# Rotary partners of q and k: found by VectorE across the halves of the partitions, in place of products with swapped weights

## The chip, the cores and the metric

The kernel runs on one core of a Trainium2 chip. The metric is the device time of one execution in microseconds, as the median of several runs. A trace of one profiled execution stands beside it.

## What is computed

Three layers in a row on 4 x 1024 tokens of 256 features (float32): a mixture of experts at half weight, attention without a mask, with 16 query heads and 4 key/value heads of 16 features each, and the mixture of experts again with the same weights. What the change touches is the rotary embedding of q and k:

```python
def _rotate_half(x):
    x1, x2 = jnp.split(x, 2, axis=-1)
    return jnp.concatenate([-x2, x1], axis=-1)
q = jnp.einsum('bsh,oh->bso', x, Wq).reshape(b, s, NH, HD).transpose(0, 2, 1, 3)
k = jnp.einsum('bsh,oh->bso', x, Wk).reshape(b, s, NKV, HD).transpose(0, 2, 1, 3)
q = q * cos + _rotate_half(q) * sin
k = k * cos + _rotate_half(k) * sin
```

So feature d of a head needs its partner, feature d + 8 or d - 8 of the same head.

## The kernel before

The tokens go in 8 groups of 512 (GROUP). Each mixture layer is a row of slots: a slot d is one step of the loop `for d in range(-1, SLOTS + ...)` that every engine runs in its own version, 24 slots to a group (PER_GROUP), 192 to a layer, 384 in all. In a slot TensorE (PE) does 12 matmuls for the gate and 12 for the up projection (`gate_or_up`, L1070) and 12 for the down projection (`down`, L1088). ScalarE (ACT) takes the tanh of the gate (L587), VectorE (DVE) forms the gated product (`gated` L834, `product` L842), GpSimd (POOL) weighs it (L514), ACT rounds it to float16 (L594) and POOL takes the rest (L519).

Other work is laid into these slots by tables. `VISIT` gives each slot from d = 64 (FIRST) to about d = 310 two, sometimes three, visits of the attention: in a visit PE makes two score products for the maximum (L1100), which DVE reduces (L857), and two for the exponential (L1112), which ACT takes (L617). Every second visit (odd v, `quad_at`) also begins with the products with the values (L1131). `EVENTS` gives slots an event: transposes, logits, and the joins, which make q, k and v of one group. The joins of group g stand in slots 24 (g + 1) + 8 and on (P_JOIN = 8): before the change seven of them, q block 0, q block 0 with swapped weights, q block 1, the same swapped, k, k swapped, v. A q or k join is 6 matmuls of 512 columns (L1042 for q, L1045 for k). Each is an event at the end of its slot on PE and on DVE. The joins of g = 0 and 1 lie ahead of the attention, those of g = 2 to 7 inside it.

An event's product needs a PSUM bank. Ahead of the attention it is B_O, which is used by nothing else there. Inside it the bank is B_U, that of the up projection (`event_bank`), so that the up half of the next slot first waits until DVE has taken the join (`pe.wait_ge(*taken[b])` in `gate_or_up`). Between the two PE has one gate half (12 matmuls) and one visit.

q and k then take this way: DVE writes `rb`, ACT rounds it to `qo_hi` (`rope_high`, L601), POOL takes the rest (`rope_low`, L501), SP stores both to HBM (`store_block`), and for each unit u of batch and key head SP loads them back (`load`, L410 and L414), 12 DMAs to a unit, each for 16 partitions. The queue of SP is in order: spread (the weights of the experts, L372), store_block, store_values, load, rows. The first load stands at d = 64, and PE's first visit needs it in the same slot.

DVE's program in a slot is: visit, gated, product, visit, then a piece of a layer norm if the slot has one (`norm_of`, in slots 9 to 12 of a group: 4 bn_stats, bn_aggr, the Newton step, the 4 normalising ones), then the event.

Of the kernel before, what the change touches and what calls it, by code (L numbers as in the profile page):

```python
# [16 lines left out]
P = 128  # L17
# [15 lines left out]
QB = 2  # L33
# [79 lines left out]
JOINS = 2 * (QB + 1) + 1  # L113
# [53 lines left out]
def build(nc, x, wgu, wd, wg, wq, wk, wv, wo, ident_c, ktab_c, kneg_c, out):  # L167
    with ExitStack() as ctx:
# [14 lines left out]
        WQ = [sb(f"WQ{h}", [P, KT, 2 * QB, P], F16) for h in range(2)]  # L183
        WK = [sb(f"WK{h}", [P, KT, 2, K_ROWS], F16) for h in range(2)]
# [14 lines left out]
        pad = sb("pad", [P, 1])  # L199

# [36 lines left out]
        n_small = [KT * EXPERTS, KT * 2 * QB * P, KT * 2 * K_ROWS, KT * KV * HD, KT * HID]  # L237
# [109 lines left out]
        def _(sp):  # L347
# [53 lines left out]
            def load(u):  # L401
# [47 lines left out]
            for d in range(-1, SLOTS + 3):  # L449
# [35 lines left out]
        def _(pool):  # L485
# [51 lines left out]
            for d in range(-1, SLOTS + 2):  # L537
# [3 lines left out]
                if 1 <= k <= GROUPS and s in (10, 12, 14):  # L541
                    rope_low(k - 1, s // 2 - 5)
# [19 lines left out]
        def _(act):  # L562
# [33 lines left out]
            def rope_high(g, blk):  # L596
                n, rows = 3 * g + blk, P if blk < QB else K_ROWS
                act.wait_ge(j_taken, JOINS * g + 2 * blk + 2)
# [53 lines left out]
            for d in range(-1, SLOTS + 2):  # L652
# [7 lines left out]
                if 1 <= k <= GROUPS:  # L660
                    if s == 6:
                        rows_high(norm_of_join(k - 1))
                    if s in (10, 12, 14):
                        rope_high(k - 1, s // 2 - 5)
# [16 lines left out]
        def _(dve):  # L681
# [125 lines left out]
            def join(g, piece, bank):  # L807
                dve.wait_ge(j_done, JOINS * g + piece + 1)
                J = PS[:, bank, :]
                if piece < JOINS - 1:  # L810
                    blk, swapped = divmod(piece, 2)
                    n, m = P if blk < QB else K_ROWS, 3 * g + blk
# [484 lines left out]
```

## Time and profile before

| | |
|---|---|
| median of 3 runs | 2366.85 us (2366.6 to 2366.93) |
| profiled execution | 2365.77 us, its span 2364.0 us |
| PE busy | 2279.1 us, 96% of the span |
| DVE busy | 1570.8 us, 66% |
| ACT busy | 1236.7 us, 52% |
| POOL busy | 1050.9 us, 44% |

The busy time of an engine is the time in which one of its instructions runs. PE's own matmuls overlap, so that the price of a matmul on the path is the distance from one start to the next and not its duration. An engine that is idle costs nothing unless PE waits for it.

### The profile page before, as it was taken

To read this page: it belongs to the slowest core of one execution; us is meant where nothing else is said; L and a number is where in the kernel's file an instruction comes from. 1 tells how busy PE (TensorE), PEld (TensorE's weight loads), DVE (VectorE), ACT (ScalarE), POOL (GpSimd) and SP (SyncE) were. 2 spreads that over 40 slices of the span, in tenths; PEclk is the share of its full clock that TensorE was granted. 3 is DMA by queue.
4 is the path that set the end of the run, shared out by engine and by line. 5 is a ranking of instruction groups with operands and counts; after the bars stand their busy time and mean duration, and the time that the engine had idled before them with its cause. 6 is when DMAs were issued, how large, how long until landed. Compare 5 with 4: busy or idle time off the path is not lost.

```text
span 2364.0 us, 48461 instructions
## 1 busy us (share of the span) xinstructions
PE 2279.1 (96%) x19616; PEld 1517.4 (64%) x19616; DVE 1570.8 (66%) x3107; ACT 1236.7 (52%) x1966; POOL 1050.9 (44%) x863
## 2 busy tenths in 40 slices
PE   0899999999999999999999999999999999999999
PEld 0788875555555556556555555555655665688887
DVE  7656558877777777777777776776776763354543
ACT  3333332466665666666566566656666656633332
POOL 0666663443443443344334343433433434366665
PEclk9999999999999999999999999999999999999999
DMA  5210111011011011001101001010010000011010
GB/s 203 77 36 29 36 48 49 10 26 41 17 31 42 15 34 30 27 22 41 29 19 51 20 22 36 23 33 19 22 30 22 13 30 19 15 33 29 19 38 19
DMA packets 96343, 80.24 MB, mean 34 GB/s; under 512 B 40308, under 2 KB 88692, under 8 KB 95736
## 3 DMA queue, kind: packets, MB, share of 16 engines
q1 hardware_dynamic: 95976, 77.11, 11.4%
q8 instruction: 155, 2.54, 0.4%
q14 instruction: 68, 0.56, 0.1%
q10 hardware_dynamic: 144, 0.03, 0.0%
HBM read 64.25 MB, written 12.85 MB: 33 GB/s over the span
## 4 chain that ended last, share of the span: by engine, by line
PE 92%; DVE 6%; issue 1%; SPq 0%; ACT 0%; DMA 0%; POOL 0%; POOLq 0%; DVEq 0%; ACTq 0%
PE PS L1070 42%; PE PS L1088 21%; PE PS L1100 11%; PE PS L1131 11%; PE PS L1042 2%; DVE arena L857 1%; PE PS L1112 1%; PE PS L1017 1%; PE PS L1045 1%; PE PS L1172 1%; PE PS L1158 1%; DVE arena L834 0%; DVE amax L698 0%; PE PS L1026 0%; DVE WGU L709 0%
## 5 line engine op out<-in xcount | busy, mean ns | idle before, releaser
L1070 PE MATMUL PS<-XT,WGU 128*128 128x256 f16 x9216 | 1117.1, 274 | 48.9 <-DVE WGU L709 32.0
L1070 PEld LDWEIGHTS PS<-XT,WGU 128*128 128x128 f16 x9216 | 875.0, 98 | 279.8 <-issue 131.9
L519 POOL TENSOR_TENSOR arena<-arena 128x512 f16<-128x512 f32 x384 | 447.3, 1165 | 1197.4 <-ACT arena L594 1197.4
L857 DVE TENSOR_REDUCE arena<-PS 128x1 f32<-128x512 f32 x1024 | 657.7, 684 | 369.6 <-PE PS L1100 367.6
L617 ACT ACTIVATE arena<-PS,fac 128x512 f32<-128x512 f32 x1024 | 647.4, 685 | 236.2 <-PE PS L1112 234.9
L587 ACT ACTIVATE arena<-PS,fac 128x512 f32<-128x512 f32 x384 | 264.0, 688 | 760.6 <-PE PS L1070 760.6
L1088 PE MATMUL PS<-WD,arena 128*128 128x256 f16 x4608 | 568.0, 273 | 1.8 <-POOL arena L519 1.6
L1088 PEld LDWEIGHTS PS<-WD,arena 128*128 128x128 f16 x4608 | 432.3, 98 | 141.5 <-issue 89.9
L514 POOL TENSOR_TENSOR arena<-arena 128x512 f32<-128x512 f32 x384 | 492.9, 1284 | 47.0 <-DVE arena L842 45.6
L834 DVE SCALAR_TENSOR_TENSOR arena<-arena,PS 128x512 f32<-128x512 f32 x384 | 261.0, 680 | 281.2 <-ACT arena L587 280.7
L1100 PE MATMUL PS<-arena 48*128 48x512 f16 x1024 | 311.9, 382 | 7.4 <-DMA arena<-k_scratch 4.6
L1112 PE MATMUL PS<-arena 50*128 50x512 f16 x1024 | 308.6, 381 | 0.0
L842 DVE SCALAR_TENSOR_TENSOR arena<-arena,PS 128x512 f32<-128x512 f32 x384 | 263.7, 687 | 33.8 <-PE PS L1070 17.9
L1131 PE MATMUL PS<-arena 128*32 128x512 f32 x2048 | 272.7, 605 | 0.0
L594 ACT ACTIVATE arena<-arena 128x512 f16<-128x512 f32 x384 | 241.3, 628 | 6.1 <-POOL arena L514 6.1
L1100 PEld LDWEIGHTS PS<-arena 48*128 48x128 f16 x1024 | 58.1, 94 | 269.1 <-issue 210.6
L575 ACT ACTIVATE XT<-PS 128x1024 f16<-128x1024 f16 x48 | 49.2, 1024 | 57.7 <-PE PS L1017 57.7
L1131 PEld LDWEIGHTS PS<-arena 128*32 128x32 f32 x2048 | 40.3, 108 | 53.9 <-issue 29.0
L1112 PEld LDWEIGHTS PS<-arena 50*128 50x128 f16 x1024 | 56.8, 94 | 21.0 <-issue 17.8
L1017 PE MATMUL PS<-ident,XS 128*128 128x128 f16 x384 | 30.2, 223 | 20.4 <-ACT XS L570 15.7
L496 POOL TENSOR_TENSOR XS<-XN,XS 128x1024 f16<-128x1024 f32 x23 | 49.0, 2130 | 0.0
L737 DVE TENSOR_SCALAR XN<-X,mv,rstd 128x256 f32<-128x256 f32 x96 | 48.7, 567 | 0.0
(115 smaller groups left out, 835.0 us busy)
## 6 DMA issues: line engine op xcount, KB each, us to landing
arena<-ce_scratch SPq DMA_DIRECT2D x256, 128.0 KB, 3.3
arena<-wgu SPq DMA_DIRECT2D x2, 3072.0 KB, 16.1
arena<-q_scratch SPq DMA_DIRECT2D x96, 64.0 KB, 2.2
arena<-ktab_c SPq DMA_DIRECT2D x16, 256.0 KB, 4.1
q_scratch<-arena SPq DMA_DIRECT2D x32, 128.0 KB, 1.7
out<-X SPq DMA_DIRECT2D x8, 512.0 KB, 3.0
X<-wd SPq DMA_DIRECT2D x1, 3072.0 KB, 26.3
X<-x SPq DMA_DIRECT2D x1, 3072.0 KB, 15.4
```

What stands on the lines that cost most here:

```text
L514: pool.tensor_tensor(t, t, c, ALU.mult).then_inc(w_done, 1)
L519: pool.tensor_tensor(hs[1][:, d % HS, :], tw[d % 2], hs[0][:, d % HS, :], ALU.subtract).then_inc(lo_done, 1)
L587: act.activation(z_f, PS[:, B_G, :], ACT.Tanh, scale=F_TANH).then_inc(z_done, 1)
L617: act.activation(pex[:, v % RING * 2 + half, :], PS[:, B_EXP + half, :], ACT.Exp, scale=F_EXP).then_inc(exp_done, 1)
L834: dve.scalar_tensor_tensor(z_f, z_f, 1.0, PS[:, B_G, :], ALU.add, ALU.mult).then_inc(v_done, 1)
L842: dve.scalar_tensor_tensor(tw[d % 2], z_f, G_U_UP, PS[:, B_U, :], ALU.mult, ALU.mult).then_inc(t_done, 1)
L857: dve.tensor_reduce(mx[:, half * REP * QT + c:half * REP * QT + c + 1], PS[:, B_MAX + half, :], AX_X, ALU.max).then_inc(max_taken, 1)
L1070: ins = pe.matmul(PS[:, b, j * HALF_G:(j + 1) * HALF_G], WGU[w][:, kt, part * CHUNKS + c + j, :], XT[r][:, k % 2, kt, half * HALF_G:(half ...
L1088: ins = pe.matmul(PS[:, B_Y, i * HID:(i + 1) * HID], hs[r][:, d % HS, at:at + P], WD[w][:, d % PER_HALF * 2 + j, :], start=(first and j == ...
L1100: pe.matmul(PS[:, B_MAX + half, :], qst[64 * par:64 * par + 48, slot, i, t * P:(t + 1) * P], kst[64 * par:64 * par + 48, slot, half * 512: ...
L1112: pe.matmul(PS[:, B_EXP + n % 2, :], kst[64 * par:64 * par + 50, slot, k * P:(k + 1) * P], qst[64 * par:64 * par + 50, slot, head // 2, ha ...
L1131: ins = pe.matmul(PS[32 * head:32 * head + 32, B_O, :], vst[:, u % 2, k, :], pex[:, (2 * q + r // 2) % RING * 2 + r % 2, :], start=(k == 0 ...
```

## The change

The swapped products go. The rows of Wq and Wk are laid out so that the first halves of the heads of a block lie in the lower half of the partitions and the second halves in the upper one; a partner is then 64 partitions away (32 for k). DVE multiplies by the cosine as before, makes the two partner halves from the other half of the partitions into a new tile `turned` in SBUF, and adds. Seven joins become four, in slots 8 to 11; rope_high and rope_low move to slots 9, 10, 11, the stores to slots 10, 11, 12 (and 13 for v). Since a head's features now lie in two places of the scratch, each load becomes 24 DMAs of 8 partitions in place of 12 of 16. WQ and WK are half as wide, and so are their transfer and their splitting into high and low halves at the start.

```diff
-JOINS = 2 * (QB + 1) + 1
+JOINS = QB + 2
@@
-        WQ = [sb(f"WQ{h}", [P, KT, 2 * QB, P], F16) for h in range(2)]
-        WK = [sb(f"WK{h}", [P, KT, 2, K_ROWS], F16) for h in range(2)]
+        WQ = [sb(f"WQ{h}", [P, KT, QB, P], F16) for h in range(2)]
+        WK = [sb(f"WK{h}", [P, KT, K_ROWS], F16) for h in range(2)]
@@
+        turned = sb("turned", [P, GROUP])
@@ load
-                    for r, h in enumerate((0, 0, 1)):
-                        sp.dma_start(qst[64 * par + 16 * r:64 * par + 16 * r + 16, slot, :, :],
-                                     q_d[h, b, 64 * j:64 * j + 64, :]
-                                     .rearrange("(i q d) n -> q d i n", i=2, q=2)[par]).then_inc(q_in[slot], 16)
-                    for r, h in enumerate((0, 1, 0)):
-                        sp.dma_start(kst[64 * par + 16 * r:64 * par + 16 * r + 16, slot, :],
-                                     k_d[h, b, 16 * j:16 * j + 16, :]).then_inc(q_in[slot], 16)
+                    for s in range(2):
+                        at = j // 2 * P + 64 * s + 32 * (j % 2)
+                        for r, h in enumerate((0, 0, 1)):
+                            to = 64 * par + 16 * r + 8 * s
+                            sp.dma_start(qst[to:to + 8, slot, :, :], q_d[h, b, at:at + 32, :]
+                                         .rearrange("(i q d) n -> q d i n", i=2, q=2)[par]).then_inc(q_in[slot], 16)
+                        for r, h in enumerate((0, 1, 0)):
+                            to = 64 * par + 16 * r + 8 * s
+                            sp.dma_start(kst[to:to + 8, slot, :],
+                                         k_d[h, b, 32 * s + 8 * j:32 * s + 8 * j + 8, :]).then_inc(q_in[slot], 16)
@@ SP's program
-                    if s in (11, 13, 15):
-                        store_block(k - 1, s // 2 - 5)
-                    if s == 15:
+                    if s in (10, 11, 12):
+                        store_block(k - 1, s - 10)
+                    if s == 13:
                         store_values(k - 1)
@@ join on DVE
-                    if not swapped:
-                        if blk == 0:
-                            dve.wait_ge(tab_in, 32 * (g + 1))
-                        if m:
-                            dve.wait_ge(qo_lo_done, m)
-                        dve.scalar_tensor_tensor(rb[0:n, :], J[0:n, :], HALF, kcos[0:n, :], ALU.mult, ALU.mult)\
-                           .then_inc(j_taken, 1)
-                        dve.wait_ge(j_taken, JOINS * g + piece + 1)
-                    else:
-                        link(dve.scalar_tensor_tensor(J[0:n, :], J[0:n, :], HALF, ksin[0:n, :], ALU.mult, ALU.mult))
-                        dve.tensor_tensor(rb[0:n, :], rb[0:n, :], J[0:n, :], ALU.add).then_inc(j_taken, 1)
+                    link.many((
+                        dve.scalar_tensor_tensor(rb[0:n, :], J[0:n, :], HALF, kcos[0:n, :], ALU.mult, ALU.mult),
+                        dve.scalar_tensor_tensor(turned[0:n // 2, :], J[n // 2:n, :], -HALF, ksin[n // 2:n, :],
+                                                 ALU.mult, ALU.mult),
+                        dve.scalar_tensor_tensor(turned[n // 2:n, :], J[0:n // 2, :], HALF, ksin[0:n // 2, :],
+                                                 ALU.mult, ALU.mult)))
+                    dve.tensor_tensor(rb[0:n, :], rb[0:n, :], turned[0:n, :], ALU.add).then_inc(j_taken, 1)
```

How instructions move is seen best in the programs of the engines. On DVE, around the first joins of group 0 (the tiles `kcos`, `ksin` and `rb` are parts of `arena`, PS is PSUM), there stood before:

```order
L818 SCALAR_TENSOR_TENSOR arena<-PS,arena 128x512
L834 SCALAR_TENSOR_TENSOR arena<-arena,PS 128x512
L842 SCALAR_TENSOR_TENSOR arena<-arena,PS 128x512
L741 BN_STATS stats<-X 128x6 x4
L822 SCALAR_TENSOR_TENSOR PS<-PS,arena 128x512
L823 TENSOR_TENSOR arena<-arena,PS 128x512
```

and there stands now, in the same two slots:

```order
L821 SCALAR_TENSOR_TENSOR arena<-PS,arena 128x512
L822 SCALAR_TENSOR_TENSOR turned<-PS,arena 64x512
L824 SCALAR_TENSOR_TENSOR turned<-PS,arena 64x512
L826 TENSOR_TENSOR arena<-arena,turned 128x512
L837 SCALAR_TENSOR_TENSOR arena<-arena,PS 128x512
L845 SCALAR_TENSOR_TENSOR arena<-arena,PS 128x512
L745 BN_STATS stats<-X 128x6 x4
L821 SCALAR_TENSOR_TENSOR arena<-PS,arena 128x512
L822 SCALAR_TENSOR_TENSOR turned<-PS,arena 64x512
```

A join takes one or two instructions of DVE before and four now, and DVE gives the bank back behind the fourth; the add, which read PSUM, now reads SBUF alone.

On PE, from the last join of q to the v join of group 0, there stood before:

```order
L1042 MATMUL PS<-XT,WQ 128x512 x6
L1070 MATMUL PS<-XT,WGU 128x256 x24
L1088 MATMUL PS<-WD,arena 128x256 x12
L1045 MATMUL PS<-XT,WK 64x512 x6
L1070 MATMUL PS<-XT,WGU 128x256 x24
L1088 MATMUL PS<-WD,arena 128x256 x12
L1045 MATMUL PS<-XT,WK 64x512 x6
L1070 MATMUL PS<-XT,WGU 128x256 x24
L1088 MATMUL PS<-WD,arena 128x256 x12
L1051 MATMUL PS<-WV,XT 128x64 x24
```

and now:

```order
L1044 MATMUL PS<-XT,WQ 128x512 x6
L1072 MATMUL PS<-XT,WGU 128x256 x24
L1090 MATMUL PS<-WD,arena 128x256 x12
L1047 MATMUL PS<-XT,WK 64x512 x6
L1072 MATMUL PS<-XT,WGU 128x256 x24
L1090 MATMUL PS<-WD,arena 128x256 x12
L1053 MATMUL PS<-WV,XT 128x64 x24
```

The v join comes three slots earlier, and three slots of the group have no join.

On SP, from the stores of group 1 to the first load, there stood before (ten more rows of 3 DMAs follow up to the end of unit 2):

```order
L390 DMA q_scratch<-arena 128x512 x4
L372 DMA arena<-ce_scratch 32x4x256 x4
L392 DMA k_scratch<-arena 64x512 x2
L399 DMA v_scratch<-arena 128x4x32 x4
L410 DMA arena<-q_scratch 16x2x1024 x3
L414 DMA arena<-k_scratch 16x1024 x3
```

and now:

```order
L391 DMA q_scratch<-arena 128x512 x4
L393 DMA k_scratch<-arena 64x512 x2
L400 DMA v_scratch<-arena 128x4x32 x4
L373 DMA arena<-ce_scratch 32x4x256 x4
L414 DMA arena<-q_scratch 8x2x1024 x3
L418 DMA arena<-k_scratch 8x1024 x3
```

The stores have moved ahead of the spread, which now lies between them and the load, and the load has twice as many DMAs, each of half the size.

## Rows read from the trace of the kernel before

**Rows 1.** The page: busy us of the engines; the chain that ended last by engine.

```profile
PE 2279.1 (96%) x19616; PEld 1517.4 (64%) x19616; DVE 1570.8 (66%) x3107; ACT 1236.7 (52%) x1966; POOL 1050.9 (44%) x863
...
PE 92%; DVE 6%; issue 1%; SPq 0%; ACT 0%; DMA 0%; POOL 0%; POOLq 0%; DVEq 0%; ACTq 0%
```

**Rows 2.** Waits of PE: who, for whom, us in total, times, longest.

```profile
PE PS L1100 <- DMA arena<-k_scratch: 4.6, 1, 4.6
...
PE PS L1070 <- DVE arena L823: 3.4, 3, 1.6
```

**Rows 3.** Timeline of PE ahead of the attention: start us, length us, what.

```profile
203.56 1.46 PE L1042 MATMUL PS<-XT,WQ 128*128 128x512 f16 x6
204.85 2.78 PE L1070 MATMUL PS<-XT,WGU 128*128 128x256 f16 x24
...
208.78 1.46 PE L1042 MATMUL PS<-XT,WQ 128*128 128x512 f16 x6
...
230.24 1.48 PE L1045 MATMUL PS<-XT,WK 128*64 128x512 f16 x6
231.65 0.61 PE L1070 MATMUL PS<-XT,WGU 128*128 128x256 f16 x4
```

**Rows 4.** Groups of instructions on DVE: busy us, mean ns.

```profile
L822 DVE SCALAR_TENSOR_TENSOR PS<-PS,arena 128x512 f32<-128x512 f32 x16 | 11.2, 699 | 2.9 <-PE PS L1042 2.6
...
L823 DVE TENSOR_TENSOR arena<-arena,PS 128x512 f32<-128x512 f32 x16 | 11.0, 686 | 0.5
...
L822 DVE SCALAR_TENSOR_TENSOR PS<-PS,arena 64x512 f32<-64x512 f32 x8 | 5.5, 692 | 11.2 <-PE PS L1045 11.2
```

**Rows 5.** Timeline inside the attention: a join, then a visit without values.

```profile
638.22 1.46 PE L1042 MATMUL PS<-XT,WQ 128*128 128x512 f16 x6
...
639.78 0.70 DVE L822 SCALAR_TENSOR_TENSOR PS<-PS,arena 128x512 f32<-128x512 f32 x1 [0.40 <-PE PS L1042]
640.52 0.69 DVE L823 TENSOR_TENSOR arena<-arena,PS 128x512 f32<-128x512 f32 x1
...
641.45 1.49 PE L1070 MATMUL PS<-XT,WGU 128*128 128x256 f16 x12
```

**Rows 6.** Timeline of PE: a join, and the up products behind a visit with values.

```profile
477.29 1.46 PE L1042 MATMUL PS<-XT,WQ 128*128 128x512 f16 x6
...
481.53 1.49 PE L1070 MATMUL PS<-XT,WGU 128*128 128x256 f16 x12
```

**Rows 7.** Timeline: a join that DVE takes late, and PE's wait.

```profile
653.72 1.46 PE L1042 MATMUL PS<-XT,WQ 128*128 128x512 f16 x6
...
657.08 0.70 DVE L822 SCALAR_TENSOR_TENSOR PS<-PS,arena 128x512 f32<-128x512 f32 x1
...
658.64 1.47 PE L1070 MATMUL PS<-XT,WGU 128*128 128x256 f16 x12 [1.62 <-DVE arena L823]
```

**Rows 8.** Timeline: DVE with two SBUF inputs beside a running POOL.

```profile
253.49 1.27 POOL L514 TENSOR_TENSOR arena<-arena 128x512 f32<-128x512 f32 x1
253.66 1.24 DVE L773 TENSOR_TENSOR pr<-pr,r 128x128 f32<-128x128 f32 x1
```

**Rows 9.** Timeline of SP and PE around the first load.

```profile
336.10 1.48 PE L1045 MATMUL PS<-XT,WK 128*64 128x512 f16 x6
...
345.53 1.39 SPq L410 DMA_DIRECT2D arena<-q_scratch  x3
346.54 1.47 PE L1070 MATMUL PS<-XT,WGU 128*128 128x256 f16 x12
...
352.64 0.59 PE L1100 MATMUL PS<-arena 48*128 48x512 f16 x2 [4.63 <-DMA arena<-k_scratch]
353.16 2.72 PE L1070 MATMUL PS<-XT,WGU 128*128 128x256 f16 x12
```

**Rows 10.** Splitting of weights at the start, by width.

```profile
L709 DVE SCALAR_TENSOR_TENSOR WQ<-arena,up,WQ 128x1024 f16<-128x1024 f32 x1 | 1.3, 1285 | 0.0
...
L709 DVE SCALAR_TENSOR_TENSOR WO<-arena,up,WO 128x512 f16<-128x512 f32 x1 | 0.8, 752 | 0.0
```

More of the change, by code:

```diff
@@ L236, in build @@
         n_gu, n_d = KT * 2 * CHUNKS * P, CHUNKS * HID
[L237 removed]
+        n_small = [KT * EXPERTS, KT * QB * P, KT * K_ROWS, KT * KV * HD, KT * HID]
         st_gu, st_g, st_q, st_k, st_v, st_o = carve([(n, F32) for n in [n_gu] + n_small])
@@ L540, in _ @@
                     low(d)
-                if 1 <= k <= GROUPS and s in (10, 12, 14):
-                    rope_low(k - 1, s // 2 - 5)
+                if 1 <= k <= GROUPS and s in (9, 10, 11):
+                    rope_low(k - 1, s - 9)
                 if d + 1 < SLOTS:
@@ L597, in rope_high @@
                 n, rows = 3 * g + blk, P if blk < QB else K_ROWS
-                act.wait_ge(j_taken, JOINS * g + 2 * blk + 2)
+                act.wait_ge(j_taken, JOINS * g + blk + 1)
                 if n >= 2:
@@ L662, in _ @@
                         rows_high(norm_of_join(k - 1))
-                    if s in (10, 12, 14):
-                        rope_high(k - 1, s // 2 - 5)
+                    if s in (9, 10, 11):
+                        rope_high(k - 1, s - 9)
                 if 0 <= k < PREPS - 1:
@@ L810, in join @@
                 if piece < JOINS - 1:
-                    blk, swapped = divmod(piece, 2)
-                    n, m = P if blk < QB else K_ROWS, 3 * g + blk
-                    if not swapped:
-                        if blk == 0:
-                            dve.wait_ge(tab_in, 32 * (g + 1))
-                        if m:
-                            dve.wait_ge(qo_lo_done, m)
-                        dve.scalar_tensor_tensor(rb[0:n, :], J[0:n, :], HALF, kcos[0:n, :], ALU.mult, ALU.mult)\
-                           .then_inc(j_taken, 1)
-                        dve.wait_ge(j_taken, JOINS * g + piece + 1)
-                    else:
-                        link(dve.scalar_tensor_tensor(J[0:n, :], J[0:n, :], HALF, ksin[0:n, :], ALU.mult, ALU.mult))
-                        dve.tensor_tensor(rb[0:n, :], rb[0:n, :], J[0:n, :], ALU.add).then_inc(j_taken, 1)
+                    n, m = P if piece < QB else K_ROWS, 3 * g + piece
+                    if piece == 0:
+                        dve.wait_ge(tab_in, 32 * (g + 1))
+                    if m:
+                        dve.wait_ge(qo_lo_done, m)
+                    link.many((
[5 more added lines that the diff above has]
+                    dve.tensor_tensor(rb[0:n, :], rb[0:n, :], turned[0:n, :], ALU.add).then_inc(j_taken, 1)
                 else:
@@ L1037, in join @@
                 if piece < JOINS - 1:
-                    blk, swapped = divmod(piece, 2)
                     for m, (a, b) in enumerate(PASSES):
                         for kt in range(KT):
-                            if blk < QB:
+                            if piece < QB:
                                 ins = pe.matmul(PS[:, bank, :], WQ[a][:, kt, piece, :], XT[b][:, slot, kt, :],
@@ L1044, in join @@
                             else:
-                                ins = pe.matmul(PS[0:K_ROWS, bank, :], WK[a][:, kt, swapped, :], XT[b][:, slot, kt, :],
+                                ins = pe.matmul(PS[0:K_ROWS, bank, :], WK[a][:, kt, :], XT[b][:, slot, kt, :],
                                                 start=(m == 0 and kt == 0), stop=(m == 2 and kt == KT - 1))
@@ L1143, in visit @@
                         pe.wait_ge(const_rows, 32)
-                    pe.wait_ge(q_in[u % QKV], 192 * (u // QKV + 1))
+                    pe.wait_ge(q_in[u % QKV], 384 * (u // QKV + 1))
                 if 0 <= v < VISITS and v % FILLS == 0:
@@ L1249, in rope_tables @@
     cos, sin = np.cos(ang).T.astype(np.float32), np.sin(ang).T.astype(np.float32)
-    sin = np.concatenate([-sin[:HD // 2], sin[HD // 2:]])
-    return np.stack([np.tile(cos, (8, 1)), np.tile(sin, (8, 1))])
+    cos, sin = cos[:HD // 2], sin[:HD // 2]
+    return np.stack([np.tile(cos, (16, 1)), np.tile(sin, (16, 1))])
 def layouts(a):
-    swap = (np.arange(HD) + HD // 2) % HD
     def on_partitions(w):
@@ L1264, in layouts @@
     down = a["L0_ffn_down_proj"].transpose(0, 2, 1).reshape(-1, HID)[rows].reshape(CHUNKS, P, HID)
-    q = a["L0_attn_Wq"].reshape(HEADS, HD, HID)
-    k = a["L0_attn_Wk"].reshape(KV, HD, HID)
+    q = a["L0_attn_Wq"].reshape(QB, HEADS // QB, 2, HD // 2, HID).transpose(0, 2, 1, 3, 4)
+    k = a["L0_attn_Wk"].reshape(KV, 2, HD // 2, HID).transpose(1, 0, 2, 3)
     return {
@@ L1271, in layouts @@
         "wg": on_partitions(a["L0_ffn_gate_weight"]),
-        "wq": on_partitions(np.stack([q.reshape(QB, P, HID), q[:, swap].reshape(QB, P, HID)], axis=1)
-                            .reshape(-1, HID)),
-        "wk": on_partitions(np.concatenate([k.reshape(-1, HID), k[:, swap].reshape(-1, HID)])),
+        "wq": on_partitions(q.reshape(-1, HID)),
+        "wk": on_partitions(k.reshape(-1, HID)),
         "wv": on_partitions(a["L0_attn_Wv"]),
```

## The prediction, made before the changed kernel ran

> **What bounds the kernel now.** I read the page first. PE is busy for 96% of the span and holds 92% of the chain that ended last; the other engines are at 44 to 66% [rows 1]. Then the list of PE's waits: apart from the start of the program, where PE waits for the weights to be split, it waits for hardly anything. Two entries are touched by the change: one wait of 4.6 us for the first load of q and k, and three waits, 3.4 us together, for the add that ends a swapped join on DVE [rows 2]. So nearly all of what PE no longer does comes off the time, unless it is given back as new waits, and the question is what PE meets where the joins now stand. For this I read the timeline around joins, once ahead of the attention and at several groups inside it.
>
> **What is removed from PE.** A slot ahead of the attention shows the price: the join of q starts at 203.56 and the gate products at 204.85, so a q join is worth 1.29 us; for k it is 231.65 - 230.24 = 1.41 us [rows 3]. (The durations, 1.46 and 1.48 us, overlap with what follows and are not the price.) I take the same price inside the attention. Two q joins and one k join go in each of 8 groups: 8 x (2 x 1.29 + 1.41) = **-31.9 us**. The three waits for L823 lay behind swapped q joins, which exist no more: **-3.4 us**.
>
> **What is added on DVE.** A join is now three multiplications out of PSUM and an add. Of the multiplications two have 64 (32) partitions and write into the other half. The nearest rows say that the number of partitions does not count (699 ns for 128, 692 ns for 64 [rows 4]); that the written half differs from the read one is shown by no row. Below, I take no surcharge. Above, I take twice the time, +0.7 us for each of the two. I use no surcharge, since the rows of both sizes are nearest in kind. With 0.70 us each, the small gap of 0.04 us between dependent ones (639.78 + 0.70 to 640.52 [rows 5]) and 0.69 us for the add, the four last 3 x 0.70 + 0.04 + 0.69 = 2.83 us. DVE as such has room: 8 x 3 more instructions are 8 x 3 x 0.69 = 16.6 us beside 1570.8 us of 2364. It is the latency that counts.
>
> **New waits inside the attention.** There the join holds the bank of the up products. In the slot of [rows 5] DVE starts 1.56 us behind PE's start of the join (it waited 0.40 us for it), is done at 641.21, that is 2.99 us behind the start, and PE comes to the up products at 3.23 us. With four instructions DVE is done at 1.56 + 2.83 = 4.39, and PE needs about 0.14 us to see it (657.81 + 0.69 = 658.50 would be the end of the add, PE goes on at 658.64 [rows 7]). The wait is then 4.53 - 3.23 = 1.3 us where the visit in between has no values. Where it has, PE comes only at 481.53 - 477.29 = 4.24 us [rows 6], and the wait is 0.3 us if DVE is on time. It is not always: the second join stands behind the four bn_stats, and in front of it DVE had 0.40 us of idle time here [rows 5] and no more in the other groups, so that the 2.1 us that the first join now adds are passed on in part; my estimate is 0.4 us more for the second joins with values, and nothing more for those without, since there PE itself is held by 1.3 us. By the table of visits, of the 18 joins of q and k inside the attention 7 are followed by a visit without values and 11 by one with: 7 x 1.3 + 11 x 0.3 + 3 x 0.4 = 13.6 us. Two joins stand in slots with three visits and one group (the last) has two events to a slot; there DVE was late already (the worst case of before is 3.36 us behind PE's start [rows 7]), and I add 3 us for them. **+16.6 us**. Bounds: if DVE is never late and the multiplications overlap a little, 8 us; if it is 1 us later at each of the 18, 35 us.
>
> **Ahead of the attention** the four instructions lie in a bank of their own. PE's slot with a join is 208.78 - 203.56 = 5.22 us [rows 3]; DVE needs 2.83 for the join and, at 0.69 each for this width [rows 4], 1.4 for gated and product, which leaves 1.0 us; the largest piece of a norm takes somewhat more than that, but in one slot only. What is behind the join on DVE is the gated product, which PE wants only two halves later. I take **0**; without that cover it would be 0.5 us in each of two groups.
>
> **The first load.** Before, the last k join starts at 336.10; the load begins at 345.53, takes 0.46 us of SP's queue for each DMA (1.39 for 3), and PE, which could have gone on at 346.54 + 1.47 = 348.01, goes on at 352.64 [rows 9]. Now the k join stands three slots earlier, against PE's need: it gains 3 x 3.93 = 11.8 us (204.85 to 208.78 is such a slot without its join [rows 3]). Against it, the load is 24 DMAs: 12 x 0.46 = 5.5 us more, and the spread of 4 DMAs (4 x 0.46 = 1.9 us) now lies in between. The load lands 352.64 - 336.10 + 5.5 + 1.9 = 23.9 us behind the k join, and PE needs it at 11.9 + 11.8 = 23.7 us. DVE's longer join may add 0.5 us. So of the 4.63 us some 0.5 stay: -4.1 us. Behind the long idle time PE also ran slowly: 12 gate matmuls took 2.72 us in place of 1.47 [rows 9]; with 0.5 us of idle time I expect none of this, -1.3 us. **-5.4 us**, between 0 (if DMAs of half the size cost more than the row says) and -6. The later loads (units 3 to 15) take 5.5 us longer on SP but are issued nine slots ahead of need (by the tables; five for unit 4), each longer than 3.93 us; they and the spreads queued behind them stay covered.
>
> **The start.** The split of WQ is 512 wide in place of 1024: 1285 - 752 = 0.53 us [rows 10], that of WK some 0.13. The search for the maxima shrinks by as much, and may or may not be hidden behind POOL's first reduction. **-1.0 us**, between -0.6 and -2.
>
> **The sum** is -31.9 - 3.4 + 16.6 + 0 - 5.4 - 1.0 = -25.1 us. The profiled execution took 2365.77 us, and would take 2340.7; the median of the runs is 1.1 us above it, so 2341.8 us. I give **2341.5 us**, 1.0% faster.
>
> **The lock between DVE and POOL.** The add used to read PSUM and now reads rb and turned, both in SBUF. The trace shows what that can mean: a tensor_tensor of 128 columns with two SBUF inputs took 1.24 us and ended at 254.90, 0.14 us behind the POOL instruction that was running [rows 8], while L823, with 512 columns but PSUM as one input, takes 0.69 us in the mean [rows 4]. If every add inside the attention met the start of a POOL instruction of 1.27 us, that would be 18 x 1.2 = 22 us more. In the slots that I looked at POOL is idle 3.7 to 4.4 us behind PE's start of a join (its weighing ends before DVE's turn, the rest comes later), so I put nothing of it in the sum beyond the bound. The Trainium skill (SBUF — State Buffer, on the shared port pair) states that a DVE instruction with two SBUF inputs and a GpSimd instruction that reads SBUF exclude each other for the whole instruction, whichever starts first; by that rule the change buys PE time with a DVE instruction that can be shut out, and if it were always shut out the time would be 2363 us; the trace agrees with the rule at this row.
>
> **The rivals.**
> - *Four instructions with little wait, as above*: 2331 to 2352 us. Chance 0.68.
> - *The adds are shut out by POOL* in many slots, or DVE drags its lateness from join to join: 2352 to 2364. For it speaks [rows 8] and that DVE was late before at three joins; against it, that POOL is idle in most of these moments. Central time 2358. Chance 0.13.
> - *Hardly any new wait*: the multiplications overlap, and DVE catches up: 31.9 + 3.4 + 6 + 2 - 8 = 35 us, 2331 and below. Against it, that PE comes at 3.23 us and three multiplications alone end at 3.66. Chance 0.07.
> - *Writing into the other half costs double*: 1.4 us more at each of 18 joins, 25 us: no change, 2367. No row speaks for it. Chance 0.05.
> - *The clock of PE falls at the new waits*, the case on the other side: after the idle 4.63 us of the first load 12 matmuls took 1.25 us longer [rows 9]. If that happened behind each of the 18 joins, for two such stretches each, it would be 18 x 2 x 1.25 = 45 us, 2387 us; it decides from 0.7 us a join on. Against it: behind the 1.62 us of idle time in [rows 7] the 12 matmuls took 1.47 us, as always, and the new waits are shorter than that. Chance 0.04, and 0.03 for other losses.
>
> **How the numbers follow.** About 0.2%, 4.7 us, is what a measurement of this kernel can tell from no change. Faster: 0.68 + 0.07 + 0.13 = 0.88, with a little of the doubled write 0.89; within 0.2%: 0.05; slower: 0.06. The range leaves out the last two rivals, half of the third and the upper half of the second: 2329 to 2357 us.
>
> **What the profile will show.** L1042 and L1045 (now L1044 and L1047) with 96 and 48 matmuls; the two cross-half multiplications at about 0.69 us each; among PE's waits one group that dwarfs the old ones, gate or up products waiting for the add of the join, some 15 us in 10 to 18 cases, the longest about 2 to 3 us; the wait for the first load at 0 to 1.5 us and no slow stretch behind it; adds of 0.6 to 0.7 us, the longer ones each beside a POOL instruction. I would be wrong if the cross-half writes are much dearer, if the wait for the load stays as it was because half-sized DMAs are no cheaper to land, or if DVE's lateness reaches other waits of PE, those for the maxima (L857) above all.

## The result: 1.2% faster, and the profile after

The changed kernel took 2338.36 us in the median (2336.99 to 2339.75) against 2366.72 us for the kernel before on the same chips, a ratio of 0.988 (95% interval 0.9864 to 0.9896). The profiled execution took 2338.99 us with a span of 2336.9 us, 27.1 us less than the 2364.0 of before. The forecast was 2341.5 us.

The page of the changed kernel (span, busy time by engine, shares of the chain):

```profile
span 2336.9 us, 48308 instructions
...
PE 2247.6 (96%) x19472; PEld 1504.5 (64%) x19472; DVE 1579.8 (68%) x3131; ACT 1236.0 (53%) x1966; POOL 1051.5 (45%) x863
...
PE 91%; DVE 7%; issue 1%; ACT 0%; DMA 0%; POOL 0%; POOLq 0%; DVEq 0%; ACTq 0%
```

PE lost 144 matmuls and 31.5 us of busy time against [rows 1], and is still the bound. PE's waits (who, for whom, us in total, times, longest):

```profile
PE PS L1072 <- DVE arena L826: 11.2, 14, 2.2
...
PE PS L1102 <- DVE arena L860: 2.2, 10, 0.3
PE PS L1072 <- DVE arena L830: 1.9, 2, 1.2
```

The wait for the load and that for L823, both in [rows 2], are gone. In their place stand 14 waits for the add of a join (L826) and two for the v join (L830), 13.1 us together, all inside the attention. Two waits of 0.36 us for X (L852), ahead of the attention, are new as well. What one of them is made of shows in the timeline, DVE and PE around the first join of the fourth group, a slot without values as in [rows 5]:

```profile
614.28 0.69 DVE L821 SCALAR_TENSOR_TENSOR arena<-PS,arena 128x512 f32<-128x512 f32 x1 [1.64 <-PE PS L1044]
615.01 0.69 DVE L822 SCALAR_TENSOR_TENSOR turned<-PS,arena 64x512 f32<-64x512 f32 x1
615.73 0.69 DVE L824 SCALAR_TENSOR_TENSOR turned<-PS,arena 64x512 f32<-64x512 f32 x1
616.45 0.69 DVE L826 TENSOR_TENSOR arena<-arena,turned 128x512 f32<-128x512 f32 x1
```

```profile
612.79 1.46 PE L1044 MATMUL PS<-XT,WQ 128*128 128x512 f16 x6
...
617.29 1.47 PE L1072 MATMUL PS<-XT,WGU 128*128 128x256 f16 x12 [1.19 <-DVE arena L826]
```

DVE starts 1.49 us behind the start of the join, is done at 617.14, and PE goes on 0.15 us later, 1.19 us late. The two multiplications that write into the other half take what any other of that width takes.

The first load (SP and PE), against [rows 9]:

```profile
328.59 0.95 SPq L414 DMA_DIRECT2D arena<-q_scratch  x3
329.58 0.97 SPq L418 DMA_DIRECT2D arena<-k_scratch  x3
```

```profile
338.34 1.47 PE L1072 MATMUL PS<-XT,WGU 128*128 128x256 f16 x12
339.75 0.60 PE L1102 MATMUL PS<-arena 48*128 48x512 f16 x2
```

A DMA of half the size takes SP 0.33 us in place of 0.46 (from one row to the next, for 3 DMAs), and PE comes to its first visit without waiting. SP is done with the 24 DMAs of the first unit at 337.70. Before the change PE went on 1.5 us behind the end of SP's last DMA for that unit; with the same delay the load is done some 0.5 us ahead of the visit at 339.75 (an estimate from these rows). One place is new: in the sixth group DVE takes the second join late, PE is idle for 2.21 us, and runs slowly behind it. PE's timeline, and PE's busy time and granted clock (1.00 is full speed, 2.4 GHz) in that stretch and the next:

```profile
967.95 2.72 PE L1072 MATMUL PS<-XT,WGU 128*128 128x256 f16 x12 [2.21 <-DVE arena L826]
```

```profile
967.95:971.60 3.65, 3.65 (x20) 1.78 (x20) 2.34 (x4) 0.52 (x1) 2.07 (x3) 0.57 0.21 72
971.60:974.00 2.40, 2.40 (x21) 1.34 (x18) 1.71 (x8) 1.26 (x2) 1.20 (x1) 1.00 0.00 0
```

**Where the 27.1 us are.** Removed products -31.9; waits for L823 -3.4; the load's wait -4.6 and the slow stretch behind it some -1.6; the start -0.6 (the first gate products begin at 55.82 in place of 56.38); new waits for joins +13.1, for X +0.7; the slow stretch at 968 us, 3.65 us at 0.57 of full speed, +1.6. The sum is -26.7 us. The start is uncertain by more than its size: in the traces of the changed kernel and its variants the first gate products begin between 55.36 and 57.25 us. What is the same in all of them is PE's wait for the split of the weights, 31.3 to 31.4 us in place of 32.0.

### The profile page after: what moved, and what is told of

Its sections match the earlier page's. It is cut to its first block, busy times and chain, and to the rows that moved or that the text cites. A ratio compares the mean times of both kernels' runs of the same rounds, so it can differ in the third digit from the quotient of the medians.

```text
span 2336.9 us, 48308 instructions
## 1 busy us (share of the span) xinstructions
PE 2247.6 (96%) x19472; PEld 1504.5 (64%) x19472; DVE 1579.8 (68%) x3131; ACT 1236.0 (53%) x1966; POOL 1051.5 (45%) x863
## 4 chain that ended last, share of the span: by engine, by line
PE 91%; DVE 7%; issue 1%; ACT 0%; DMA 0%; POOL 0%; POOLq 0%; DVEq 0%; ACTq 0%
PE PS L1072 43%; PE PS L1090 22%; PE PS L1102 11%; PE PS L1133 11%; PE PS L1114 1%; DVE arena L860 1%; PE PS L1020 1%; PE PS L1174 1%; PE PS L1044 1%; PE PS L1160 1%; PE PS L1047 0%; DVE arena L826 0%; DVE turned L824 0%; DVE turned L822 0%; DVE arena L821 0%
## 5 line engine op out<-in xcount | busy, mean ns | idle before, releaser
L1072 PE MATMUL PS<-XT,WGU 128*128 128x256 f16 x9216 | 1117.4, 274 | 57.5 <-DVE WGU L713 31.4
L860 DVE TENSOR_REDUCE arena<-PS 128x1 f32<-128x512 f32 x1024 | 658.1, 685 | 352.7 <-PE PS L1102 351.1
L837 DVE SCALAR_TENSOR_TENSOR arena<-arena,PS 128x512 f32<-128x512 f32 x384 | 261.2, 680 | 278.5 <-ACT arena L591 278.0
L845 DVE SCALAR_TENSOR_TENSOR arena<-arena,PS 128x512 f32<-128x512 f32 x384 | 263.8, 687 | 34.1 <-PE PS L1072 17.9
L741 DVE TENSOR_SCALAR XN<-X,mv,rstd 128x256 f32<-128x256 f32 x96 | 43.6, 515 | 0.0
```

The lines of the kernel that those rows point to most:

```text
L837: dve.scalar_tensor_tensor(z_f, z_f, 1.0, PS[:, B_G, :], ALU.add, ALU.mult).then_inc(v_done, 1)
L845: dve.scalar_tensor_tensor(tw[d % 2], z_f, G_U_UP, PS[:, B_U, :], ALU.mult, ALU.mult).then_inc(t_done, 1)
L860: dve.tensor_reduce(mx[:, half * REP * QT + c:half * REP * QT + c + 1], PS[:, B_MAX + half, :], AX_X, ALU.max).then_inc(max_taken, 1)
L1072: ins = pe.matmul(PS[:, b, j * HALF_G:(j + 1) * HALF_G], WGU[w][:, kt, part * CHUNKS + c + j, :], XT[r][:, k % 2, kt, half * HALF_G:(half ...
```

## Experiments

The theory: the gain is that of the removed products and of the load that is no longer late, and what is given back is the time for which a join holds the bank of the up products. The rivals: the lateness of DVE as such is what costs; the two cross-half multiplications are free or, at the other end, cost their full time; the place of the joins does not matter. The waits and timelines are those of one profiled execution of each kernel, which is not always near its median; where that matters the text says so. All of these kernels were timed beside the kernel before, which took 2366.55 to 2366.95 us in the median.

### The changed kernel again

> The changed kernel once more, beside the three variants that follow, so that differences of a few us can be read on one chip. Any theory: 2336 to 2340 us, and among PE's waits again some 11 us for the add that ends a q or k join and 2 us for the v join.

2338.9 us (2337.09 to 2339.78), with the same waits for joins: L826 11.2 us in 14 cases, L830 1.9 us in two. It is the measure for the others.

### The bank back behind the third multiplication

```diff
-                    link.many((
+                    for ins in (
                         ...
-                                                 ALU.mult, ALU.mult)))
+                                                 ALU.mult, ALU.mult)):
+                        ins.then_inc(j_free, 1)
+                    dve.wait_ge(j_free, 3 * m + 3)
@@ PE
-                    taken[bank] = (j_taken, JOINS * n + j + 1)
+                    taken[bank] = (j_free, 9 * n + 3 * j + 3) if j < JOINS - 1 else (j_taken, JOINS * n + j + 1)
```

> One thing is changed: DVE gives the bank of a q or k join back behind the third multiplication, which is the last instruction that reads it, and no longer behind the add. My theory (what the new joins cost PE is the time for which the bank of the up products is held): each of the waits for the add becomes up to 0.72 us shorter, those of 0.20 to 0.50 us vanish, and the 2.21 us one falls to 1.5 us, so that PE's clock does not fall behind it. From the list of waits that is 7 us, and 1.25 us for the clock: 8 us faster than the changed kernel, 2330 us. Rival (DVE's lateness as such, through the gated product or the maxima, holds PE, and the bank is only what the profile names): less than 2 us faster, as DVE does the same work in the same order. Second rival (the waits move to the v join or to the next slot): 3 to 5 us faster, with longer waits for the v join or for the maxima.

2330.91 us (2330.78 to 2331.4), ratio 0.9849 (0.9834 to 0.9864): 8.0 us under the changed kernel, as forecast. PE's waits:

```profile
PE PS L1075 <- DVE turned L825: 4.1, 7, 1.5
...
PE PS L1075 <- DVE arena L833: 2.1, 2, 1.5
```

The waits for q and k joins went from 11.2 to 4.1 us; the longest, now 1.48 us, has no slow stretch behind it. In the slot shown above PE's wait went from 1.19 to 0.47 us, which is the add's 0.72:

```profile
616.12 1.47 PE L1075 MATMUL PS<-XT,WGU 128*128 128x256 f16 x12 [0.47 <-DVE turned L825]
```

DVE does the same work in the same order here, so its lateness as such is not what PE paid these 8 us for; the time for which the bank is held is. The first rival falls. The 6.2 us of waits that are left are those in which DVE's third multiplication, or its turn at the v join, still comes later than PE.

### Two of the four instructions left out

```diff
-                        dve.scalar_tensor_tensor(rb[0:n, :], J[0:n, :], HALF, kcos[0:n, :], ALU.mult, ALU.mult),
-                        dve.scalar_tensor_tensor(turned[0:n // 2, :], J[n // 2:n, :], -HALF, ksin[n // 2:n, :],
-                                                 ALU.mult, ALU.mult),
-                        dve.scalar_tensor_tensor(turned[n // 2:n, :], J[0:n // 2, :], HALF, ksin[0:n // 2, :],
-                                                 ALU.mult, ALU.mult)))
-                    dve.tensor_tensor(rb[0:n, :], rb[0:n, :], turned[0:n, :], ALU.add).then_inc(j_taken, 1)
+                        dve.scalar_tensor_tensor(rb[0:n, :], J[0:n, :], HALF, kcos[0:n, :], ALU.mult, ALU.mult),))
+                    dve.tensor_tensor(rb[0:n, :], rb[0:n, :], rb[0:n, :], ALU.add).then_inc(j_taken, 1)
```

> The two multiplications that write across the halves are left out, and the add takes the cosine part twice; q and k have no sine part, everything else is as in the changed kernel. It prices the cross-half work of DVE. My theory: DVE holds the bank 1.44 us shorter, as long as a swapped join did before; the waits for the add fall from 11.2 us to under 2 us, the clock no longer falls, and the time is 10 to 12 us under the changed kernel, 2326 to 2328 us. Rival (the two multiplications cost nothing since DVE has idle time): no difference. Rival (they cost their own time, 48 x 0.69 = 33 us, as if DVE were the bound): 2305 us.

2326.83 us (2326.12 to 2328.99), 12 us under the changed kernel, at the middle of the forecast. Of the waits for the add one is left:

```profile
PE PS L1068 <- DVE arena L826: 2.7, 2, 2.1
...
PE PS L1068 <- DVE arena L822: 0.8, 1, 0.8
```

(L822 is the add here, L826 the v join.) The list explains the 12 us: 10.4 us of waits for the add, the two waits for X (0.7) and the slow stretch (1.6) are gone, and the waits for the v join grew by 0.8. The two multiplications are neither free nor do they cost their own 33 us: DVE is not the bound, and they cost what they hold the bank beyond PE's arrival.

### The join ahead of the down products

```diff
+                early = bool(EVENTS[d]) and EVENTS[d][0][0] == "join" and EVENTS[d][0][2] < JOINS - 1 \
+                    and event_bank(d, 0) == B_U
+                if early:
+                    event(d, 0)
                 if 0 <= d - 1 < SLOTS:
                     down(d - 1)
                 ...
-                if EVENTS[d]:
+                if EVENTS[d] and not early:
                     event(d, 0)
```

> One thing is changed, on PE alone: inside the attention a q or k join stands ahead of the slot's down products in place of behind them, so that 12 more matmuls (1.3 us) lie between the join and the up products that need its bank. My theory: the waits for the add fall from 11.2 us to some 3 us, but where the visit in front of the join has no values PE comes to the join before the gated product of the slot is done and waits up to 0.4 us for L842's counterpart, some 4 us in all: 4 to 7 us faster than the changed kernel, 2331 to 2334 us. Rival (PE's order does not matter since DVE is the one that is behind): the waits for the add go down and those for the gated product go up by as much, no difference.

A miss: 2342.65 us (2339.88 to 2343.91), 3.8 us slower than the changed kernel. PE's waits:

```profile
PE PS L1072 <- DVE arena L826: 9.2, 7, 3.8
...
PE PS L1072 <- DVE arena L830: 2.7, 2, 2.1
...
PE PS L1044 <- DVE arena L845: 2.1, 4, 0.5
...
PE PS L1047 <- DVE arena L845: 0.9, 2, 0.5
```

The wait for the gated product (L845) came as foreseen, 3.0 us. The waits for the add became fewer (7 for 14) but longer, 9.2 us and not the 3 that I expected. The longest, 3.79 us, is in the three-visit slot of the sixth group: PE now issues the join ahead of the third visit, and DVE still takes that visit's maxima first. (In the same place DVE's add takes 0.97 us in place of 0.69, beside a POOL instruction that ends 0.54 us before it.) To move one engine's place of a join without the other's only moves the wait. Behind two of the waits PE ran slowly, where the changed kernel has one such place:

```profile
642.78 2.56 PE L1072 MATMUL PS<-XT,WGU 128*128 128x256 f16 x12 [2.07 <-DVE arena L830]
...
972.49 2.72 PE L1072 MATMUL PS<-XT,WGU 128*128 128x256 f16 x12 [3.79 <-DVE arena L826]
```

### Both together

> Both together: the bank back behind the third multiplication, and the join ahead of the down products. My theory: the waits for q and k joins are gone but for one or two, what is left is the wait of the join for the gated product, up to 4 us, and 1 to 2 us for the v join: 2328 to 2331 us. If the join's wait for the gated product is as large as the waits that are left with the early release alone, the two together are no faster than the early release alone.

2337.31 us (2335.68 to 2340.42), 6.4 us slower than the early release alone. PE's waits:

```profile
PE PS L1075 <- DVE turned L825: 4.3, 5, 2.8
...
PE PS L1075 <- DVE arena L833: 2.7, 2, 2.1
...
PE PS L1047 <- DVE arena L848: 2.1, 4, 0.5
PE PS L1050 <- DVE arena L848: 1.9, 3, 0.9
```

The waits for the multiplications are 4.3 us as with the early release (4.1), and 4.0 us of waits for the gated product (L848) are added. This is slower than the 2328 to 2331 us that I expected. The second branch of the expectation, that the two together are no faster than the early release alone, holds, and more: with the bank back early there is nothing left for PE's order to win.

### The join ahead of the layer norm's piece, on DVE

```diff
+                first = bool(EVENTS[d]) and EVENTS[d][0][0] == "join"
+                if first:
+                    event(d, 0)
                 if 1 <= k <= GROUPS and 2 <= s < 6:
                 ...
-                if EVENTS[d]:
+                if EVENTS[d] and not first:
                     event(d, 0)
```

> On DVE alone a join stands ahead of the piece of the layer norm in its slot and not behind it. My theory: the second joins of a group, which stand behind four bn_stats (1.4 us), are no longer late: the wait of 2.21 us in the sixth group falls to 1.3 us and the clock does not fall behind it, the waits of 0.36 to 0.50 us at second joins fall to 0.2 us. The others are bound by PE's own products and stay. 2 to 4 us faster than the changed kernel. Rival (a late norm piece makes something else late): no difference or slower.

A miss: 2342.87 us (2342.4 to 2344.87), 4 us slower. The 2.21 us wait did fall to 1.19 and the slow stretch went, but the others took its place:

```profile
PE PS L1075 <- DVE arena L837: 10.2, 6, 4.8
PE PS L1075 <- DVE arena L826: 9.5, 14, 1.2
...
PE PS L1105 <- DVE arena L860: 4.4, 17, 0.5
...
PE PS L1056 <- DVE arena L845: 2.2, 1, 2.2
PE PS L1093 <- DVE X L852: 1.7, 2, 0.8
```

Against the changed kernel L826 saves 1.7 us, while L837 (the gated product's first half) costs 1.6, the maxima (L860) 2.2, L845 2.2 and L852 1.0 more. The waits for the v join (1.9 us) and the slow stretch (1.6) are gone too. My reading, which no run tests by itself: a norm piece in front of a join ran while DVE waited for PE's products anyway; behind the join it stands in the way of the next slot's work. The single wait of 2.24 us for L845 shows one such knot: ahead of it two instructions of DVE with 32 columns (L869, L870), which take under 0.2 us each in the changed kernel, take 1.09 us each beside POOL instructions of 1.16 and 1.15 us. About 2 us of the difference are in no entry of this list.

### The joins in the old slots

```diff
+JOIN_AT = (9, 11, 13, 14)
...
-                at[k * PER_GROUP + P_JOIN + j].append(("join", k - 1, j))
+                at[k * PER_GROUP + JOIN_AT[j]].append(("join", k - 1, j))
```

with rope_high, rope_low and the stores in slots 10 to 15 as before.

> The four joins of a group stand where the swapped ones stood: q in slots 9 and 11, k in 13, v in 14, with rope_high, rope_low and the stores in their old slots. Everything else is the changed kernel. It takes the earlier first load away and leaves the removed products. My theory (the earlier place is worth the wait for the first load): PE waits again for the load of q and k at the first visit, and longer than before the change, since the load has 24 DMAs at 0.33 us (8.1 us in place of 5.5): 6 to 8 us, and runs at low clock behind it, 1.3 us. The joins are two slots apart, but 11 of 18 now have a visit without values behind them in place of 7: some 15 us of waits for the add in place of 11. Together 9 to 14 us slower than the changed kernel, 2347 to 2352 us. Rival (the place of the joins does not matter, all of the gain is the removed matmuls): within 3 us of the changed kernel.

2361.27 us (2357.86 to 2363.62): 22.4 us slower than the changed kernel, where 9 to 14 were expected. The direction is right, the size is not. PE's waits:

```profile
PE PS L1073 <- DVE arena L827: 20.6, 16, 3.8
...
PE PS L1073 <- DVE arena L838: 11.2, 6, 4.0
...
PE PS L1103 <- DMA arena<-k_scratch: 7.1, 1, 7.1
```

The load costs what I said. The waits for the add are 20.6 us where I had put 15, since I had not looked at what stands in front of a join in slot 11. I had also put nothing for the first two groups' waits for the gated product and for X, 3.9 us more than in the changed kernel (two new waits of 1.06 us for L838, and two of 1.25 us for L853 in place of 0.36). Some 3 us are in no trace: the profiled execution, 2357.86 us with a mean granted clock of 0.998, was the fastest of ten; the other nine took 2359.08 to 2363.62 us at 0.994 to 0.996. DVE and POOL at the longest, 3.78 us (the timelines of the two engines):

```profile
650.76 1.97 DVE L758 TENSOR_TENSOR rstd<-nw,rs 128x4 f32<-128x4 f32 x1
652.77 0.69 DVE L822 SCALAR_TENSOR_TENSOR arena<-PS,arena 128x512 f32<-128x512 f32 x1
...
654.93 1.42 DVE L827 TENSOR_TENSOR arena<-arena,turned 128x512 f32<-128x512 f32 x1
```

```profile
650.59 2.13 POOL L533 TENSOR_TENSOR arena<-arena 128x1024 f16<-128x1024 f32 x1
654.65 1.15 POOL L524 TENSOR_TENSOR arena<-arena 128x512 f16<-128x512 f32 x1 [1.94 <-ACT arena L599]
```

A Newton step of 4 columns takes 1.97 us beside a POOL instruction of 2.13, and the join's add takes 1.42 us beside one that ends at 655.80; it then needs 0.55 us more. This is the lock of [rows 8] at work on the add.

### The first two groups in the old slots

> The changed kernel with the joins of the first two groups alone, those ahead of the attention, in the old slots 9, 11, 13 and 14; the other six groups have them in slots 8 to 11. It parts what the joins in old slots cost (22 us over the changed kernel, with all groups moved) into the first load and the rest. My theory, from the trace of that run: the wait for the first load 7.1 us, slow clock behind it 3.4 us, waits for the gated product and for X in these two groups 2.1 + 1.8 us: 14 us over the changed kernel, 2350 to 2354 us. Rival (most of it was lateness of DVE inside the attention, the slots are what matters there): less than 7 us over it.

The edit is the last one, for g < 2 alone. 2352.53 us (2350.41 to 2354.39), in the middle of the forecast: 14 us of the 22 belong to the two groups ahead of the attention. PE's waits and PE's row behind the load:

```profile
PE PS L1110 <- DMA arena<-k_scratch: 7.1, 1, 7.1
...
PE PS L1098 <- DVE X L860: 2.5, 2, 1.2
```

```profile
353.54 2.74 PE L1080 MATMUL PS<-XT,WGU 128*128 128x256 f16 x12
```

So, with 24 DMAs to a load, the place of the first two groups' joins is worth 14 us, nearly half of what the removed products are; in the changed kernel it came along with their removal. The waits inside the attention are those of the changed kernel, to the tenth (11.2 us in 14 cases for the add, 1.9 us for v). The other 9 us of the run before this one belong to the joins inside the attention. By the traces, the waits for the add are 9.4 us longer there and those for the v join, 1.9 us, are gone. The two profiled executions differ by only 2.9 us of span, so this split rests on the medians: one was the fastest of its ten and the other the second slowest of its four, and they reached the first gate products at 55.36 and 57.25 us.

### The kernel before with one matmul for each swapped join

```diff
-                    for m, (a, b) in enumerate(PASSES):
-                        for kt in range(KT):
+                    passes = PASSES[:1] if swapped else PASSES
+                    kts = 1 if swapped else KT
+                    for m, (a, b) in enumerate(passes):
+                        for kt in range(kts):
                         ...
```

> The kernel before, in which each swapped join has one matmul in place of six (the partner is then wrong): all events, all instructions of DVE and all DMAs stay. It prices the removed products alone. My theory (PE is the bound, a matmul of 512 columns is worth 1.29 / 6 = 0.215 us): 24 x 5 x 0.215 = 25.8 us faster than the kernel before, 2341 us, less a little where the joins come back sooner than DVE can take them, so 2341 to 2344 us; the wait for the first load stays at 4.6 us. Rival (the matmuls lay in the shadow of DVE's work): less than 15 us faster.

A miss: 2352.09 us (2350.93 to 2354.59), 14.9 us faster than before and not 23 to 26. The rival (the products in DVE's shadow, under 15 us) is met in its number (14.9), but the list of waits shows another cause:

```profile
PE PS L1073 <- DVE arena L823: 9.7, 9, 2.7
...
PE PS L1103 <- DMA arena<-k_scratch: 4.7, 1, 4.7
```

```profile
652.00:656.00 4.00, 3.98 (x22) 1.60 (x24) 2.35 (x4) 0.53 (x1) 2.57 (x3) 0.59 0.27 84
980.00:984.00 4.00, 3.93 (x20) 1.74 (x20) 2.40 (x4) 0.60 (x2) 2.86 (x3) 0.57 0.19 66
1338.00:1342.00 4.00, 3.92 (x22) 1.54 (x24) 2.41 (x4) 0.59 (x1) 3.12 (x3) 0.60 0.23 71
```

6.3 us went to longer waits for L823 (9.7 for 3.4), and behind three of them, of 2.70, 1.85 and 2.13 us, PE ran at 0.57 to 0.60 of full speed for 4 us: 3 x 1.6 = 5 us. With these, 25.8 is cut to 14.5 us against 14.9 in the medians. That this agrees so well is in part luck: the waits and the slow stretches are those of the profiled execution, the slowest of the four, and it gained only 11.2 us of span over that of before. Of the 3.3 us between, 1.3 are a later start (the first gate products at 57.64 in place of 56.38) and 1.3 small waits (two for X in L849 0.7, L889 0.4, L897 0.2); the rest is open. So this run bears out that the removed products are worth about what they take on PE, to some 3 us. When a join is 1.1 us shorter on PE and not on DVE, some of it comes back as waiting. The changed kernel does better than this by what its new slots bring at the first load.

### The early release again, and with it other slots inside the attention

> The early release once more, as a measure for the run that follows: 2330 to 2332 us.

2331.3 us (2330.94 to 2332.26), ratio 0.9852 (0.9836 to 0.9869).

> The early release, and inside the attention the joins of a group in slots 8, 10, 13 and 14 (q, q, k, v), so that none stands behind the four bn_stats of slot 9 or the Newton step of slot 11; the first two groups stay in slots 8 to 11. My theory: of the 6.2 us that PE still waits for joins with the early release, the two v joins (2.1 us) and the late second join of the sixth group (1.5 us) go, and 8 in place of 7 q and k joins are followed by a visit without values (0.5 us): 2 to 3 us under the early release alone, 2328 to 2329 us. Rival: the maxima of the rows (max_rows) or the adding of outputs hold DVE in the new slots, and the waits come back there: no difference.

```diff
+def join_at(g):
+
+    return (8, 9, 10, 11) if g < 2 else (8, 10, 13, 14)
```

2327.74 us (2327.35 to 2328.59), ratio 0.9837 (0.9822 to 0.9851), 3.6 us under the early release in the same session; the ranges don't touch. PE's waits for joins:

```profile
PE PS L1083 <- DVE arena L848: 8.1, 4, 4.2
...
PE PS L1083 <- DVE turned L833: 3.2, 8, 0.5
```

The v joins are no longer waited for, and no wait for a join is over 0.5 us (the four for L848 lie at the start of the program). This is the fastest version, 38.9 us or 1.6% under the kernel before.

## Why the prediction was right, point by point

- **What is removed from PE** (-31.9 us): held. PE's busy time fell by 31.5 us, and the three waits for L823 went. On the path itself the price is borne out to some 3 us, by the kernel before with one matmul for each swapped join.
- **What is added on DVE** (2.83 us a join, no surcharge for the other half): held. In the slot shown the four take 614.28 to 617.14, 2.86 us. The rival of a doubled write falls: 0.69 us for each of them. The join's instructions took 66.0 us together, for 49.5 before, as forecast; DVE's busy time as a whole rose by 9.0 us only, since others became shorter (the normalising one, L741, 43.6 us for 48.7).
- **New waits inside the attention** (+16.6 us): 13.1 us. Without values the size was right: 1.3 us forecast, and six of the seven measured 1.05 to 1.25 us; With values it was too high: 0.3 us each and 0.4 more for three second joins, 4.5 us in all, against 2.0; seven of eleven measured 0.20 to 0.50 us, the other four nothing that the list shows, and PE waited 0.16 to 0.30 us longer for the second joins than for the first ones. The seventh without values was the late one in the three-visit slot, 2.21 us. Two more things balanced in part: I had put 3 us for late places, which came to 1.0; and I had not thought of the v join, whose bank is waited for as well (1.9 us) when the Newton step makes DVE late.
- **Ahead of the attention** (0): held, PE has no wait for a join there; two waits of 0.36 us for X are new.
- **The first load** (-5.4 us): -6.2. I took the issue of a half-sized DMA for as dear as that of a whole one; it is 0.33 us in place of 0.46, so that the load is done in time, by about 0.5 us. The run with the first two groups in the old slots shows that this term is real and that the slots decide it: there the same 24 DMAs make PE wait for 7.1 us, more than the 4.6 of before.
- **The start** (-1.0 us): -0.6 in the two traces, the lower bound, but the start of the same work differs by up to 1.9 us from trace to trace. PE's wait for the split fell by 0.6 to 0.7 us in every one, which is the narrower split (0.53 + 0.13 by the prediction). That the shorter search for maxima is hidden is likely, but not shown.
- **The lock between DVE and POOL**: absent from the adds in the changed kernel, where the add takes at most 694 ns in 24 cases, as argued from POOL's idle time at that moment. It is no fiction: in the kernel with the old slots one add took 1419 ns, and in three other variants the longest took 974 to 1244 ns. The Trainium skill (SBUF — State Buffer, on the shared port pair) has the rule that the second of the two waits until the first is done; the rows of that run agree with it, since the add goes on for 0.55 us behind the end of the POOL instruction. In none of these kernels was the lock worth 22 us, the price that the prediction gives it if every add is shut out.
- **The clock**: I put this at 0.04 as a loss behind each join. It fell behind one wait, the longest, and cost about 1.6 us. That a wait for a join can be followed by a slow stretch was right; what brings it about stays open (see the end). In the variants it decided more: by the trace it is 5 of the 11 us that the run with one matmul fell short of its forecast, and part of what the early release gained.
- **The total**: 2341.5 us forecast, 2338.36 measured. The mechanism held, and that the number came this close is partly luck: the new waits for joins were 3.5 us under the forecast and the load 0.8 us better, and against them stand 1.6 us of slow clock, 0.7 us for X and 0.4 us less at the start.

## What to carry to other kernels

When work moves from the engine that bounds to one with idle time, price the latency at the shared buffer and not the busy time: here 24 more instructions on DVE, 16.5 us of its time, brought PE 13.1 us of waits for a PSUM bank that the next product needs; and of a join's four instructions two, 33 us of DVE's time, were worth 12 us. Give the buffer back behind its last reader rather than behind the last instruction of the group; that alone was worth 8 us. And look at what the freed slots do to a transfer that was late: 6 us came from there.

## What was not expected of the hardware

- An idle PE and its clock. The granted clock fell to about half, 1.2 GHz, behind waits of 3.79, 2.70, 2.21, 2.13, 2.07 and 1.85 us, but not behind those of 1.84 us for X (L900) in the changed kernel, nor behind one of 2.06 us in the kernel with two of the four instructions, nor behind one of 2.78 us with both edits together, nor, in the kernel with the old slots, behind 2.20, 2.48 and 3.78 us: the next 12 matmuls took 1.47 us. So the length of a single wait does not tell it. The times of the changed kernel spread over 2.7 us, those with the early release over 0.6 us. The mean granted clock of each execution goes with this: in the first four executions of the changed kernel the two at 0.998 took 2338.99 and 2339.75 us and the two at 0.999 took 2336.99 and 2337.73; with the early release all are at 0.999. But only one execution of each kernel has a trace, so it is not shown that slow stretches in the others are the reason.
- The issue of a DMA of 8 partitions and 2 x 1024 elements took SP 0.33 us, of 16 partitions 0.46 us.

```profile
656.49 1.47 PE L1073 MATMUL PS<-XT,WGU 128*128 128x256 f16 x12 [3.78 <-DVE arena L827]
```
